# Expert table in three pieces, the last two batches routed together inside the expert loop

## What is computed

```python
x = x + attention(layernorm(x))
x = x + moe0(layernorm(x))          # 8 experts, top 2, weighted, plus a shared part and a norm
x = x + retrieval_attention(layernorm(x))
x = x + moe1(layernorm(x))          # 8 experts, top 2, not weighted

probs = softmax(flat @ gate_w)      # (2048, 8)
_, idx = top_k(probs, 2)
for e in range(8):
    out += chosen(e) * (act(flat @ w1[e] + b1[e]) @ w2[e] + b2[e])   # 128 -> 512 -> 128
```

## Time and profile before

| | us |
|---|---|
| three runs | 632.91, 641.87, 645.01 |
| their median | 641.87 |
| the profiled execution, device time | 632.19 |
| its span, first to last instruction | 630.5 |
| TensorE busy in it | 509.7 |
| VectorE busy | 409.7 |
| ScalarE busy | 293.1 |
| GpSimd busy | 268.2 |

### The profile page before, as it was taken

How to read it: one execution, slowest core, us unless ns; L and a number is a source line. 1 busy time by engine, 2 the same in 40 slices (tenths; PEclk the granted TensorE clock), 3 DMA queues, 4 the chain that set the end, 5 groups by cost and what they waited for, 6 DMA issues and landing times.

```text
span 630.5 us, 14217 instructions
## 1 busy us (share of the span) xinstructions
PE 509.7 (81%) x4416; PEld 409.7 (65%) x4416; DVE 409.7 (65%) x1351; ACT 293.1 (46%) x824; POOL 268.2 (43%) x358
## 2 busy tenths in 40 slices
PE   4789998999976699995066999989889684999990
PEld 3565765666544599995055767767677364989990
DVE  5778689687877664633877657756875867453333
ACT  2224553354552466765325366625444321667650
POOL 3324343336476356547000233313543645465550
PEclk9979899596997699998566779977796855999995
DMA  7998000000001222221999000000000002223216
GB/s 231 313 303 327 2 2 1 1 1 23 14 25 39 70 70 83 70 61 48 373 308 346 6 2 2 2 1 2 19 18 3 22 23 57 70 72 84 69 39 208
DMA packets 28376, 53.72 MB, mean 85 GB/s; under 512 B 4816, under 2 KB 24208, under 8 KB 27248
## 3 DMA queue, kind: packets, MB, share of 16 engines
q1 hardware_dynamic: 23216, 42.17, 21.2%
q0 software_dynamic: 4544, 9.45, 4.2%
q10 hardware_dynamic: 544, 1.20, 0.6%
HBM read 42.32 MB, written 29.81 MB: 114 GB/s over the span
## 4 chain that ended last, share of the span: by engine, by line
PE 58%; DVE 26%; issue 5%; DMA 4%; ACT 2%; POOL 2%; SPq 1%; ACTq 0%; DVEq 0%; POOLq 0%
PE ps L1989 12%; PE ps L1997 11%; DVE negm L859 4%; PE ps L2089 3%; DVE X L1362 2%; PE ps L2049 2%; PE ps L1835 2%; DMA w<-ybuf 2%; PE ps L1871 2%; PE ps L1845 2%; PE ps L2073 2%; PE ps L1980 2%; PE ps L1905 1%; PE ps L1770 1%; PE ps L1906 1%
## 5 line engine op out<-in xcount | busy, mean ns | idle before, releaser
L1569 ACT ACTIVATE probs<-ps,w1s 128x128 f32<-128x128 f32 x312 | 89.3, 370 | 48.5 <-PE ps L1989 48.3
L748 POOL DMA_INDIRECT ybuf<-yt,xg x78 | 76.8, 985 | 71.6 <-DVE yt L1116 64.3
L1989 PE MATMUL ps<-xgT,w1s 128*128 128x128 f32 x624 | 87.5, 286 | 2.3 <-ACT xgT L1560 2.1
L1989 PEld LDWEIGHTS ps<-xgT,w1s 128*128 128x128 f32 x624 | 80.1, 201 | 3.4 <-ACT xgT L1560 2.8
L1997 PE MATMUL ps<-w,probs 128*128 x624 | 82.3, 276 | 0.0
L769 POOL TENSOR_SCALAR_AFFINE_SELECT probs<-probs 128x512 f32<-128x512 f32 x64 | 39.2, 637 | 96.5 <-ACT probs L1670 96.4
L859 DVE TENSOR_REDUCE negm<-ps 128x2 f32<-128x512 f32 (+1 forms) x96 | 60.3, 685 | 25.1 <-PE ps L1822 19.4
L1997 PEld LDWEIGHTS ps<-w,probs 128*128 128x128 f32 x624 | 75.7, 192 | 0.1
L694 POOL DMA_INDIRECT xbuf<-rsc,sloti x64 | 62.4, 976 | 30.7 <-DVE sloti L988 15.2
L1483 ACT ACTIVATE probs<-ps 128x512 f32<-128x512 f32 x96 | 51.3, 601 | 35.3 <-PE ps L1845 34.6
L639 POOL TENSOR_SCALAR_AFFINE_SELECT probs<-probs 128x512 f32<-128x512 f32 x64 | 39.2, 637 | 65.4 <-ACT probs L1483 65.2
(11 more groups left out here) (280 smaller groups left out, 1129.0 us busy)
## 6 DMA issues: line engine op xcount, KB each, us to landing
xbuf<-in_c_pads SPq DMA_DIRECT2D x16, 1122.0 KB, 19.0
xg<-xbuf SPq DMA_DIRECT2D x78, 66.0 KB, 1.9
w<-in_w SPq DMA_DIRECT2D x2, 2064.0 KB, 34.0
w<-in_w SPq DMA_DIRECT2D x2, 2048.0 KB, 36.0
w<-ybuf SPq DMA_DIRECT2D x8, 512.0 KB, 5.7
ybuf<-yt,xg POOLq DMA_INDIRECT x78, 2.3
probs<-in_c_sel ACTq DMA_DIRECT2D x2, 512.0 KB, 5.5
bias<-in_b SPq DMA_DIRECT2D x2, 512.0 KB, 31.5
```

The costliest lines, as they stand in the source:

```text
L748: pool.indirect_dma_start(out=ybuf[l][:, :], out_offset=bass.IndirectOffsetOnAxis(ap=xg[n % AHEAD][:, D:D + 1].bitcast(I32), axis=0), in_= ...
L1569: ins = act.activation(hidT[n % 3][:, c * P:(c + 1) * P], ps[:, q, c * P:(c + 1) * P], ACT.Gelu if l == 0 else ACT.Relu, bias=w[:, FF + c: ...
L1989: mm = pe.matmul(ps[:, n % 2, c * P:(c + 1) * P], w[:, c * P:(c + 1) * P], xgT[n % 2][:], start=True, stop=True)
```

## The change

The groups become (0,1), (2,3), (4,5), (6,7), so that batches 6 and 7 are both the late group and are routed together in the expert stage. COUNTED becomes 1: counts are taken from group 1 on. The table is made in three pieces, of 9, 8 and 22 tiles (ENDS = 9, 17, 39), known from the counts of batches 0 to 3, 0 to 5 and all. `place_early` moves to steps 34 and 29, `stage_first` and `used_early` to 35 and 30. A count is read by a function of its own, `read_count`, at the step of the slots. The second piece is made by `place_more(l, 1, ...)` in iterations 3 to 5 of the expert loop, `used_middle` (four operations) follows in iteration 7, and the third piece comes in iterations 9 to 11, each step of the late routing one or two iterations later than before. SP waits ahead of tiles 0, 9 and 17, for the rows of batches 0 to 3, 4 and 5, 6 and 7. POOL issues all eight scatters of the late group in iteration 5, ahead of tile 5's output scatter. In the prelude `rstd0` for tiles 4 to 15 follows `moments0` at step (-1, 0).

```diff
-GROUPS = ((0, 1), (2, 3), (4, 5), (6,), (7,))
+GROUPS = ((0, 1), (2, 3), (4, 5), (6, 7))
 LATE = len(GROUPS) - 1
-COUNTED = 2
+URGENT = LATE - 1
+COUNTED = 1
-AFTER = (dict(turn=2, copy=3, gate=3, logits=4, second=5, rank=6, slots=7), dict(turn=1, copy=2, gate=2, logits=3, second=3, rank=3, slots=4))
-PLACED = (38, 33)
-EARLY = -(-(P * TOPK * TILES[COUNTED][1] - E * (P - 1)) // P)
+AFTER = 2 * (dict(turn=2, copy=3, gate=3, logits=4, second=5, rank=6, slots=7),) + (dict(turn=1, copy=2, gate=2, logits=3, second=3, rank=3, slots=4),)
+PLACED = (34, 29)
+ENDS = [-(-(P * TOPK * TILES[q][1] - E * (P - 1)) // P) for q in (COUNTED, COUNTED + 1)] + [ET]
+KNOWN = ((0, 1, 2, 3), (4, 5), (6, 7))
...
# SP, experts
-                    if n in (0, EARLY):
-                        sp.wait_ge(m["placed"], (1 if n == 0 else 2) + 1)
-                        for b in range(2, 6) if n == 0 else range(6, B):
+                    if n in (0, *ENDS[:-1]):
+                        k = (0, *ENDS[:-1]).index(n)
+                        sp.wait_ge(m["placed"], k + 1 + 1)
+                        for b in KNOWN[k]:
                             sp.wait_ge(rows_out[b % 4], rows_sent(l, b))
...
# POOL, experts
-                    if 0 <= n - LATE_ROWS < TOPK * size(LATE):
-                        t, k = divmod(n - LATE_ROWS, TOPK)
-                        ready_row(l, TILES[LATE][0] + t, LATE)
-                        scatter_row(l, TILES[LATE][0] + t, k)
+                    if n == LATE_ROWS:
+                        for t in range(*TILES[LATE]):
+                            scatter_rows(l, t, LATE)
...
# VectorE
+            def read_count(l, k, bank):
+                m = ms[l]
+                dve.wait_ge(m["counted"], k + 1 + 1)
+                dve.tensor_scalar(per_ei[:, 0, :], bank[:, 0:E], float(P - 1) if k == 2 else 0.0, None, ALU.add).then_inc(m["count_read"], 1)
+                dve.wait_ge(m["count_read"], k + 1 + 1)
...
+            def used_middle(l):
+                c = chains[l]
+                c(dve.tensor_scalar(per_e[:, 1, :], per_e[:, 3, :], float(ENDS[1] - ENDS[0]), None, ALU.min))
+                c(dve.tensor_tensor(used_to[:, 1:E + 1], used_to[:, 1:E + 1], per_e[:, 1, :], ALU.add))
+                pairs_used(c)
...
                 if (c, s) == (-1, 0):
                     dve.wait_ge(x_loaded[1], 16)
                     moments0(FIRST, NT)
-                if (c, s) == (-1, 3):
                     rstd0(FIRST, NT)
...
# VectorE, experts
-                    if n == 5:
+                    if n in (3, 4, 5):
+                        place_more(l, 1, n - 3)
+                    if n == 6:
                         take_logits(l, LATE, late)
                         choose(l, LATE, 0)
-                    if n == 6:
+                    if n == 7:
+                        used_middle(l)
                         choose(l, LATE, 1)
-                    if n == 7:
+                    if n == 8:
                         give_slots(l, LATE, ps[:, 2, :])
-                    if n == 8:
-                        place_late(l, ps[:, 3, :], 0)
-                    if n in (9, 10):
-                        place_late(l, ps[:, 3, :], n - 8)
+                    if n == 9:
+                        read_count(l, 2, ps[:, 3, :])
+                    if n in (9, 10, 11):
+                        place_more(l, 2, n - 9)
...
# TensorE, experts: turn_rows at n = 4 (was 2), gate_rows at 5 (4), older_rows at 7 (6), rank_rows at 8 (7)
```

More of the change, by code:

```diff
@@ L396, in to_scatter @@
                 t0, t1 = TILES[q]
-                per = 2 if q >= COUNTED else 1
-                n = u - u0 - AFTER[q >= COUNTED]["slots"]
+                per = 2 if q == URGENT else 1
+                n = u - u0 - AFTER[q]["slots"]
                 for t in range(t0 + per * n, t0 + per * n + per):
@@ L1809, in route_rows @@
                     bank = take("rank", q)
-                    count = take("count", q) if q == COUNTED else None
+                    count = take("count", q) if q >= COUNTED else None
                     older_rows(l, q, bank, count)
@@ L1998, in out_of_hidden @@
                     mm.then_inc(m["y_ready"], 1)
[L2000 removed]
+                late = {("rT", 0): ps[:, 2, :], ("gate", 0): ps[:, 3, :], ("gate", 1): ps[:, 2, :]}
                 def take_late(kind, q, n=0):
```

72 lines of the change are left out of this document (36 added, 36 removed).

## The result

In the comparison that the prediction was about, the changed kernel took 647.64 us (median of five executions; the lowest is 647.05, and one took 2336.26) and the kernel before 644.75: a ratio of 1.0143, with a 95% interval of [1.008, 1.0207]. I had said 622, with 608 to 635. The ratios here leave out executions that were disturbed in themselves, so they can stand a little apart from the ratio of the medians. The comparison was then repeated four times, on three chips (A, B and C; the first comparison's chip isn't recorded).

What follows compares the result with a forecast made beforehand. TensorE's expert tiles at 1.89 us bound the kernel, so only their start could be won: 1.9 + (9.4 - 1.5) + (6.6 - 1.7) = 14.7 us off 632.2 gives 617.5, or 627.0 at the median's level; forecast 622, range 608 to 635.

Steps and rivals of the forecast that it cites:

- Parts 1 and 2: Prelude: rounding of batch 1 comes 1.9 us earlier. Layer 0: the experts' first transpose comes 9.4 us earlier.
- part 3: Start of the experts in layer 1: the first transpose comes at about 525.4 instead of 532.0, 6.6 us earlier.
- part 2's note that the gathers are no obstacle: Layer 0: the first gather issues near 196 and lands near 198, ahead of the first transpose at about 201.3.
- Part 4: Expert stages: added routing work gives back 1.5 us in layer 0 and 1.7 in layer 1, between nothing and 5 each.
- Part 5: Queues in the expert stages: the eight-scatter block takes 10.1 us, leaving about 1 us of slack at tile 17; nothing lost.
- Rival (d): Expert stages: the eight scatters, run while VectorE copies weights, are stretched and gate tile 17; slower, 638.3 us; chance 0.05.
- the 3.1 us that the prediction took over from the page: Skill's figure for a transfer taking 0.62 us alone, when a float32 VectorE copy locks GpSimd out of issuing descriptors.
- The slow start that the sum kept: First stretch of the experts: TensorE's clock at 0.53 of full, 1.2 GHz, from 210.6 to 217.6, assumed to stay.
- the silent one ahead of part 4: Expert stages: one tile costs 1.89 us of TensorE and nothing else; only the time the stage begins can be won.
- two levels of one and the same course: Profiled execution 632.2 us, median 1.5% above it; the same ratio gives 617.5 or 627.0, so 622 between them.

Runs made afterwards that it cites:

- spread: The changed kernel with the eight late scatters one ahead of each of outputs 5 to 12 instead of in one block; ratio 1.0108 to the kernel before.
- prelude_only: The kernel before with only the prelude's roots moved behind the moments; ratio 0.9916 to the kernel before.
- sooner_half: The changed kernel with late routing one tile sooner and a GpSimd memset behind every second late and output scatter; 647.28 us against 642.09 before.
- gaps_before: The kernel before with a GpSimd memset behind its four late scatters and output scatters 5 to 24; 635.29 us, ratio 0.985 to the kernel before.
- gaps_all: The changed kernel with a GpSimd memset behind each late scatter and output scatters 5 to 24; 633.13 us, ratio 0.9798 to the kernel before.

## Why the prediction was wrong, point by point

**Parts 1 and 2 held in kind, part 3 for a third.** The rounding of batch 1 moved from 27.40 to 25.69 in the first profile (1.7 us, forecast 1.9). The experts of layer 0 start 6 to 10 us nearer to batch 5's residual (forecast 9.4), released by batch 7's residual; part 2's note that the gathers are no obstacle holds too. The loop of layer 1 was to be 6.6 us shorter. With both kernels on one chip it is 2.2 (A) and 2.5 us (C) shorter. The 7.0 us against the first profile are so many because the kernel before stood at 144.8 us in that one and at 140.0 and 140.3 in its two others.

**Part 4 held only where the counts are in time.** On chip A the expert stages grew by 0.8 and 0.9 us; I had given back 1.5 and 1.7, at most 5 each. In the first profile they grew by 16.3 and 14.2.

**Part 5 held, and is the reason why the block is right.** spread shows that tile 17 has about 1.5 us of slack. The block took its 1.27 us a scatter; the 64 scatters take 973 ns on average, as before (976). Rival (d), scatters stretched by VectorE's copies, is not what happened: the eight scatters of the first profile that overlap a weight copy take 1.01 us on average, at most 1.10 (on chip A thirteen do, at most 1.23). The Trainium skill ("SBUF — State Buffer", the warning on DVE blocking DMA) has GpSimd locked out while such a copy runs. A copy here takes 0.43 us, so the 3.1 us that the prediction took over from the page don't carry over to it, and its sentence that by that rule (d) would be the outcome went too far.

**On chip A the sum came out, by luck.** The two profiles there stand at spans of 616.6 and 630.9 us, 14.3 less (forecast 14.7), and by medians it is 10.8, ratio 0.978 where I had 0.977. But the terms are others. Batch 5's residual comes 8.1 us earlier (177.1 for 185.2), where the forecast had 1.9 from the prelude; prelude_only, without the new table, has it at 176.9. From there to the experts 6.2 us are gained (forecast 9.4), in the loop of layer 1 2.2 (6.6), and the stages lose 1.7 (3.2). The first term is far too large and the next two are too small. The slow start that the sum kept did stay: the first 3.7 and 6.0 us of the stages are at the half clock, 4.5 and 6.2 in the kernel before there.

**The step that failed is the silent one ahead of part 4: "39 tiles at that pace are 74 us, in each of two layers, and no edit shortens it."** That none would lengthen it I took from one profile, in which GpSimd's scatters cost nothing to anyone but GpSimd. Part 4's give-back of 1.5 and 1.7 us, at most 5 each, rests on it, and it is the term that measured 16.3 and 14.2. On chips B and C, in the first profile of the changed kernel, and in sooner_half on chip D, scatters at one per 1.27 us (one per 1.42 in sooner_half) make TensorE's counts late and stop all that waits for them. The kernel before sends four late scatters one at a time and pays about 5 us per stage (86.2 and 87.5 against 81); the change sends eight together, with three outputs piled up behind them, and since the longest of the late counts come only after the stream has stopped, the longer stream costs more: 13 to 17 us. On chip C the difference is 8.3 and 10.5 us, 18.8 together, against the 12.2 that the start (9.7) and the loop of layer 1 (2.5) gain in the same profiles. The term is missing from the sum altogether, and no rival names it: I asked whether the scatters themselves would be slow, and never what a denser stream of them does to the other engines.

**There was a sign.** The profiled execution stood at 632.2 us and the median of the runs at 641.9. I took this as two levels of one and the same course and multiplied. The kernel before on chip C takes 4.7 and 5.9 us more in its expert stages than the profile which I worked from: 10.6 us in all, which is near those 10, though that profiled execution took only 4.3 us more (636.51). That most of the first runs of the kernel before stood in the same condition as on such a chip is a conclusion; of the changed kernel its profile shows it.

## What to carry to other kernels

When a profile stands well below the median of the runs, look for the stage that has a second length before scaling. An engine off the critical path is not free: ask what rate of descriptors, scatters or semaphore traffic a reordering will make, not only when its last item is out. And if a burst of indirect scatters is behind a stall, a pause of 0.4 us between them is a cheap test and, on chips C and D, a cheap cure.

## What the runs showed of the hardware

- On chips B and C TensorE's counts were acted upon 2 to 3 us and then up to 12 us late once GpSimd had issued indirect scatters 1.27 us apart for about 2 to 4 us; those over 8 us late came 1.1 to 2.3 us after GpSimd had run out of work. On chip A the same instructions in the same order gave 0.04 us. With one scatter per 1.56 us (chips C and D, tiles 6 to 25) none was over 1.3 us late, but for 2.5 and 1.8 us in gaps_before. The rate alone isn't enough: the eight scatters that end the loop of layer 1 go out 1.27 us apart too, and in no profile is a count of tiles 0 to 2 there over 2.1 us late.
- In each profile with late counts 4 to 15 of SyncE's register instructions took 0.5 to 0.73 us; in the five without (the one that the prediction worked from, and the four of chip A) none took over 0.48. The DMA engines were not busy: their share from 236 to 252 was 0.17.
- What TensorE and SyncE wait for is not shown, and one rival was never tried: that the recording of the profile takes part in it. All times here are of executions that are traced. The five profiles without late counts hold 7,668 to 7,682 semaphore records, the other fifteen (gaps_all and gaps_before among them) 5,561 to 5,812. The missing ones are not spread evenly. In the first 120 us all twenty have 1,173 to 1,215; in the first 60 us of an expert stage the five have 1,028 to 1,312 and the fifteen 449 to 655. So the late counts stand in just those stretches, and on just those chips, where half or more of the semaphore records are missing. A lower rate of scatters is also a lower rate of such records. That the scatters' rate brings the late counts on is shown for traced executions; whether an untraced one would have them is open.
- The change of the prelude moves the rounding of batch 1 by about 2 us, but the granted clock from 40 to 80 us was 0.79 in the changed kernel's first profile and 0.93 on chip A, and the first residual of the loop came at 81.3 and 76.2 us.
